# Second cross-attention of a Perceiver block: two positions at a time on 32-row and 32-column groups of TensorE

## The reference

```python
def _L1_xattn_ref(x, context, Wq, Wkv, Wout, bout):      # x: (8, 64, 256), context: (8, 1024, 256)
    heads, dim_head = (16, 64)
    q = x @ Wq
    k, v = jnp.split(context @ Wkv, 2, axis=-1)
    q, k, v = map(split_heads, (q, k, v))
    mask = j_idx % n_q == i_idx                            # key j counts for position i if j % 64 == i
    sim = jnp.einsum('bhid,bhjd->bhij', q, k) * scale
    attn = jax.nn.softmax(jnp.where(mask, sim, max_neg), axis=-1)
    out = jnp.einsum('bhij,bhjd->bhid', attn, v)
    return out @ Wout + bout
```

## Time and profile before

| | us |
|---|---|
| three runs | 892.03, 895.23, 895.33 (median 895.23) |
| the profiled execution | 893.96 |
| its span | 892.1 |
| PE busy in it | 839.7 (94%) |
| VectorE, ScalarE, GpSimd busy | 508.0, 413.1, 105.5 |
| mean granted TensorE clock | 0.987 |

### The profile page before, as it was taken

One profiled execution on the slowest core, in us unless ns is written; L12 is line 12 of the kernel. 1 busy time (PEld: TensorE's weight loads), 2 busy tenths in 40 slices (PEclk: granted clock), 3 DMA queues, 4 the chain that ended last, 5 costly groups with the idle time before them and its releaser, 6 DMA issues.

```text
span 892.1 us, 20057 instructions
## 1 busy us (share of the span) xinstructions
PE 839.7 (94%) x7916; PEld 681.3 (76%) x7916; DVE 508.0 (57%) x1181; ACT 413.1 (46%) x821; POOL 105.5 (12%) x102
## 2 busy tenths in 40 slices
PE   5999999999889798999999999999989999779997
PEld 3788788888748697888888888887369967568885
DVE  4777877787643655555555555554355631675332
ACT  3757566676640223445545454443455641422221
POOL 2333311340000440000000000000011000400200
PEclk9999999999999799999999999999999999989999
DMA  7446644476090000023123213004516668213860
GB/s 297 188 155 213 236 178 167 150 258 202 4 397 1 2 4 1 22 121 141 55 88 141 87 54 141 0 0 155 222 48 233 238 237 342 85 35 158 369 296 25
DMA packets 25867, 128.14 MB, mean 144 GB/s; under 512 B 2360, under 2 KB 8272, under 8 KB 21712
## 3 DMA queue, kind: packets, MB, share of 16 engines
q1 hardware_dynamic: 24624, 111.51, 33.4%
q0 software_dynamic: 1184, 15.77, 4.3%
HBM read 126.75 MB, written 0.52 MB: 143 GB/s over the span
## 4 chain that ended last, share of the span: by engine, by line
PE 82%; DVE 7%; DMA 4%; issue 2%; ACT 2%; SPq 1%; POOL 1%; DVEq 0%; ACTq 0%
PE PS L387 13%; PE PS L388 12%; PE PS L389 12%; PE PS L396 5%; PE PS L697 4%; PE PS L947 3%; DMA arena<-in_bias 3%; PE PS L1149 3%; PE PS L820 3%; PE PS L966 3%; PE PS L1161 3%; PE PS L709 3%; PE PS L686 3%; PE PS L935 2%; PE PS L920 2%
## 5 line engine op out<-in xcount | busy, mean ns | idle before, releaser
L1329 ACT CAST w_h<-arena 128x768 fp32r<-128x768 f32 x64 | 53.4, 835 | 124.8 <-PE PS L389 124.8
L1689 DVE TENSOR_TENSOR w_l<-arena,w_h 128x768 fp32r<-128x768 f32 x64 | 61.2, 957 | 87.0 <-ACT w_h L1329 87.0
L387 PE MATMUL PS<-xnT_h,w_h 128*128 128x512 f32 x256 | 99.7, 390 | 0.8 <-DVE xnT_l L381 0.8
L389 PE MATMUL PS<-xnT_h,w_l 128*128 128x512 f32 x256 | 99.6, 389 | 0.0
L388 PE MATMUL PS<-xnT_l,w_h 128*128 128x512 f32 x256 | 99.6, 389 | 0.0
L1527 DVE CUSTOM_DVE_ANT_0 arena<-PS,arena 128x512 f32<-128x512 f32 x128 | 86.9, 714 | 20.7 <-PE PS L686 18.7
L1229 ACT ACTIVATE arena<-arena 128x1024 f32<-128x1024 f32 x64 | 73.5, 1150 | 9.9 <-DVE arena L1527 9.8
L697 PE MATMUL PS<-consts,arena 128*128 128x128 f32 x512 | 68.3, 277 | 0.7 <-ACT arena L1234 0.4
L697 PEld LDWEIGHTS PS<-consts,arena 128*128 128x128 f32 x512 | 55.9, 141 | 10.5 <-issue 3.6
L1696 DVE TENSOR_TENSOR arena<-PS,arena 128x512 f32<-128x512 f32 x64 | 44.3, 691 | 29.1 <-PE PS L389 27.3
L387 PEld LDWEIGHTS PS<-xnT_h,w_h 128*128 128x128 f32 x256 | 48.0, 188 | 11.2 <-DVE xnT_l L381 1.2
(11 more groups left out here) (301 smaller groups left out, 1763.2 us busy)
## 6 DMA issues: line engine op xcount, KB each, us to landing
arena<-in_bias SPq DMA_DIRECT2D x64, 512.0 KB, 4.2
arena<-in_wall SPq DMA_DIRECT2D x8, 3072.0 KB, 9.9
arena<-in_wf SPq DMA_DIRECT2D x8, 2052.0 KB, 11.2
hT<-in_ctxT SPq DMA_DIRECT2D x12, 1024.0 KB, 6.4
arena<-in_ctxT SPq DMA_DIRECT2D x4, 1024.0 KB, 6.3
arena<-in_ctxG SPq DMA_DIRECT2D x4, 1024.0 KB, 4.8
hT<-in_ctxG SPq DMA_DIRECT2D x4, 1024.0 KB, 4.8
arena<-in_w SPq DMA_DIRECT2D x2, 1024.0 KB, 6.2
```

The costliest lines, as they stand in the source:

```text
L387: pe.matmul(out, a[0], b[0], start=start, stop=False)
L389: return pe.matmul(out, a[1], b[0], start=False, stop=stop)
L1329: act.copy(w_h[:, s % 4, :], stage[s // 8 % 2][:, s % 8, :]).then_inc(sem("c_wh"), 1)
L1689: dve.tensor_tensor(w_l[:, s % 4, :], stage[s // 8 % 2][:, s % 8, :], wide(w_h[:, s % 4, :]), ALU.subtract).then_inc(sem("c_wl"), 1)
```

## The change

- `U` is laid out as half, pair of positions, then 32 columns (16 heads x 2 positions), so that the queries of a pair of positions are 32 contiguous columns. `grouped`, `Ub` and `Ub0` go, on all three engines. The copies into `U` (L1725, L1367) now write runs of two words, and L989 reads such runs.
- `sims`: per batch 32 pairs x 2 halves = 64 products of 128 rows, 32 columns of the array and 32 keys. Four pairs in turn lie in the four column groups (output partitions 32j to 32j+31). The keys come from a new array `ctxD`, in which the 32 keys of a pair are contiguous.
- One mask and softmax for a batch: VectorE adds the mask `pair` (256 columns), takes maxima, subtracts; ScalarE exponentiates all 256 columns at once; VectorE sums, takes reciprocals, multiplies.
- `sums`: 2 transposes in place of 8, one copy of 256 columns, then 64 products with 32 rows each, in the four row groups, each into its own PSUM bank (4 to 7).
- `warm` products: 3 ahead of the first scores, 3 behind them, 6 ahead of the first sums and 4 ahead of each other batch's, 3 ahead of L989.
- The loops over batches are written out.
- SP loads `wq1`, `wkT1` and `wv1` behind the last expert's weights without waiting for the last expert; `wo1` waits as before. The self-attention's weights and the first five expert blocks are asked for after L989's last product.

```diff
-    U = cd(KC, XH, TOK)
+    U = [cd(B * PP, 2 * XH), None]
...
-            sp.wait_ge(sem("c_dn"), 4 + 8 * NEXP)
             w_in(wq1, A["wq1"], "in_wq1")
             w_in(wkT1, A["wkT1"], "in_wk1")
             w_in(wv1, A["wv1"], "in_wvo1")
+
+            sp.wait_ge(sem("c_dn"), 4 + 8 * NEXP)
             w_in(wo1, A["wo1"], "in_wvo1")
...
+            for b in range(B):
+                if b >= 2:
+                    sp.wait_ge(sem("d_sim"), b - 1)
+                sp.dma_start(ctxT1[b % 2], A["ctxD"][b].rearrange("(k p) n -> p k n", p=P))\
+                  .then_inc(sem(f"d_ctxT{b % 2}"), 16)
+                if b >= 2:
+                    sp.wait_ge(sem("d_w"), b - 1)
+                sp.dma_start(ctxG[b % 2], A["ctxG"][b]).then_inc(sem(f"d_ctxG{b % 2}"), 16)
+            sp.wait_ge(sem("d_o"), FC)
             w_in(wqkv, A["wqkv"], "in_wqkv")
             w_in(wproj, A["wproj"], "in_wqkv")
...
+            def sims(b):
+                pe.wait_ge(sem(f"d_ctxT{b % 2}"), b // 2 * 16 + 16)
+                if b >= 2:
+                    pe.wait_ge(sem("d_z"), b - 1)
+                for t in range(8):
                     for dc in range(KC):
+                        for j in range(4):
+                            pp = 8 * (t % 4) + 4 * (t // 4) + j
+                            last = pe.matmul(PS[32 * j:32 * j + 32, b % 2, 32 * t:32 * t + 32], U[dc][:, b * PP + pp, :],
+                                             ctxT1[b % 2][:, dc, 32 * pp:32 * pp + 32], start=dc == 0, stop=dc == KC - 1)
+                last.then_inc(sem("d_sim"), 1)
+
+            def sums(b):
+                pe.wait_ge(sem("d_p"), b + 1)
+                if b >= 2:
+                    pe.wait_ge(sem("d_te"), b - 1)
+                for t2 in range(2):
+                    last = pe.transpose(PS[:, 2, t2 * P:(t2 + 1) * P],
+                                        Z[:, b % 2, 4 * t2:4 * t2 + 4, :].rearrange("p a b -> p (a b)"), C("ident"))
+                last.then_inc(sem("d_t"), 1)
+                pe.wait_ge(sem(f"d_ctxG{b % 2}"), b // 2 * 16 + 16)
+                pe.wait_ge(sem("d_te"), b + 1)
+                if b:
+                    for dc in range(KC):
+                        pe.wait_ge(sem(f"d_we{dc}"), b)
+                for dc in range(KC):
+                    for t2 in range(2):
+                        for j in range(4):
+                            for r in range(4):
+                                k, at = slice(32 * r, 32 * r + 32), dc * D + (4 * t2 + j) * 32
+                                last = pe.matmul(PS[:, 4 + r, at:at + 32], ctxG[b % 2][k, 4 * t2 + j, dc * P:(dc + 1) * P],
+                                                 PTx[k, b % 2, t2, 32 * j:32 * j + 32], start=True, stop=True)
+                last.then_inc(sem("d_w"), 1)
+
+            for dc in range(KC):
+                pe.wait_ge(sem(f"d_ue{dc}"), 2 * FC)
+            warm(pe, 3, 3)
+            sims(0)
+            warm(pe, 3, 3)
+            for b in range(B):
+                if b + 1 < B:
+                    sims(b + 1)
+                warm(pe, 3, 6 if b == 0 else 4)
+                sums(b)
+            warm(pe, 3, 3)
...
             exps(0)
+            for b in range(B):
+                transposed(b)
+                if b + 1 < B:
+                    exps(b + 1)
+                summed(b)
...
             scores(0)
             probabilities(0)
+            for b in range(B):
+                if b + 1 < B:
+                    scores(b + 1)
+                    probabilities(b + 1)
+                summed(b)
```

More of the change, by code:

```diff
@@ L28 @@
 XH, XD = 16, 64
-GRP, GI = 8, 8
 GM = KEYS // S
+PP = S // 2
 EPS = 1e-5
@@ L46, in const_layout @@
         "half2": ((p % 32) // DK == np.arange(2)[None, :]),
-        "group": np.where(p % GI == c % GI, 0.0, -BIG),
+        "pair": np.where(p % 2 == np.arange(32)[None, :] % 2, 0.0, -BIG),
         "upper": i > j,
@@ L464, in _ @@
             sp.wait_ge(sem("a2_o"), 2)
-            with sp.Fori(0, NEXP // 2) as i:
+            for e2 in range(2):
+                sp.dma_start(stage[e2], A["wall"][e2:e2 + 1].rearrange("a p c n -> p (a c) n"))\
+                  .then_inc(sem(f"c_w{e2}"), 16)
+            with sp.Fori(1, NEXP // 2) as i:
                 for e2 in range(2):
@@ L495, in expert_in @@
                 sp.dma_start(wblk[e], A["wf"][e * P:(e + 1) * P]).then_inc(sem(f"f_w{e // 2}"), 16)
[L497 to L501, removed]
+            for e in range(5):
                 expert_in(e)
@@ L569, in _ @@
                     .then_inc(sem("b_pool"), 1)
[L571 to L588, removed]
+            pool.wait_ge(sem("d_w"), B)
             for n in range(2):
@@ L936, in _ @@
                                   start=True, stop=True).then_inc(sem(f"d_u{dc}"), 1)
[L938 to L961, removed]
-                    pe.wait_ge(sem("d_te"), b * 2 + hf + 1)
-                    for dc in range(KC):
-                        pe.wait_ge(sem(f"d_we{dc}"), b * 2 + hf + 1)
-                        for g in range(4):
-                            last = pe.matmul(PS[:, 4 + 2 * hf + dc, g * P:(g + 1) * P],
-                                             ctxG[j][:, 4 * hf + g, dc * P:(dc + 1) * P], PTx[:, hf, g, :],
-                                             start=True, stop=True)
-                        last.then_inc(sem("d_w"), 1)
@@ L984, in _ @@
+            pe.wait_ge(sem("d_we1"), B)
             for c in range(FC):
@@ L1372, in exps @@
             def exps(b):
-                for hf in range(2):
-                    act.wait_ge(sem("d_z"), b * 2 + hf + 3)
-                    for g in range(4):
-                        last = act.activation(Z[:, hf, g, :], Z[:, hf, g, :], ACT.Exp, bias=mx1[:, hf, g:g + 1],
-                                              scale=-1.0, accum_out=rs1[:, hf, g:g + 1])
-                    last.then_inc(sem("d_e"), 1)
+                act.wait_ge(sem("d_z"), b + 1)
+                z = Z[:, b % 2].rearrange("p a b -> p (a b)")
@@ L1392, in _ @@
-            exps(0)
-            with act.Fori(1, B) as b:
-                transposed(b - 1)
-                exps(b)
-                summed(b - 1)
-            transposed(B - 1)
-            summed(B - 1)
+                act.wait_ge(sem("d_w"), b + 1)
+                for dc in range(KC):
+                    last = act.copy(U[dc][:, b * PP + 16:(b + 1) * PP, :].rearrange("p (r q) n -> p r (q n)", r=2),
+                                    PS[:, 6:8, dc * D:(dc + 1) * D])
+                last.then_inc(sem("d_we1"), 1)
@@ new lines, in probabilities @@
+            def probabilities(b):
+                z, total, inv = Z[:, b % 2], rs1[:, b % 2, :], ri1[:, b % 2, :]
+                dve.wait_ge(sem("d_e"), b + 1)
+                ch.step(dve.reduce_sum(total, z, axis=AX.X))
+                ch.step(dve.reciprocal(inv, total))
+                dve.tensor_tensor(z, z, bcast(inv, 2, (8, 32)), ALU.mult).then_inc(sem("d_p"), 1)
+            def summed(b):
+                dve.wait_ge(sem("d_w"), b + 1)
+                for dc in range(KC):
+                    last = dve.tensor_copy(U[dc][:, b * PP:b * PP + 16, :].rearrange("p (r q) n -> p r (q n)", r=2),
+                                           PS[:, 4:6, dc * D:(dc + 1) * D])
+                last.then_inc(sem("d_we0"), 1)
@@ L1933 @@
         "ctxT": ctx.transpose(0, 2, 1),
-        "ctxG": ctx.reshape(B, GM, GRP, GI, D).transpose(0, 1, 3, 2, 4).reshape(B, P, GRP, D),
+        "ctxD": ctx.reshape(B, GM, PP, 2, D).transpose(0, 4, 2, 1, 3).reshape(B, D, KEYS),
+        "ctxG": ctx.reshape(B, GM, 4, 8, 2, D).transpose(0, 2, 1, 4, 3, 5).reshape(B, P, 8, D),
         "wq0": t("L0_xattn_Wq"), "wk0": t("L0_xattn_Wk"), "wv0": t("L0_xattn_Wv"), "wo0": t("L0_xattn_Wo"),
```

114 lines of the change are left out of this document (24 added, 90 removed).

## The result

The changed kernel takes 920.3 us in the median of four runs (917.67 to 921.35), the kernel before beside it 895.28 (892.03 to 896.47). The ratio is 1.028, with an interval of 1.025 to 1.031. The forecast was 885.9 us, with a range of 881 to 902: faster by 9 us, where the kernel became slower by 25. The profiled execution of after has a span of 919.0 us against 892.1.

A forecast was written before the change was run, and what follows sets the result against it. PE was taken as the bound, busy for 94% of the span. The stage summed as 13.2 + 44.4 (six batches of 7.4) + 6.2 + 1.5 = 65.3 against 74.65 us, 9.3 less, giving 885.9 us; range 881 to 902.

The forecast's parts named there:

- Scores: Query-key products of a batch: 128 records at 8.6 ns, 1.1 us in place of 3.7.
- sums: Weighted sums of a batch: 32 rounds of four row groups loading at once, 3.55 us against 3.81 before.
- transposes: From transposes to sums in a batch, with ScalarE's copy uncovered: 0.87 us against 1.16 before.
- constants: Warm products on PE's path: 0.43 us each, four a batch 1.72 us, 43 in the stage 18.5 us.
- changes of shape: PE switching tile shape, two a batch outside of waits: 0.1 us each, an estimate, 0 to 0.2.
- floor per record: Rival: small score records cost about 30 ns whatever their size, scores 3.8 us a batch, 907 us; chance 0.09.
- loads not four abreast: Rival: full-width fp32 loads of the sums don't run four at once; two abreast 914 us, singly 970; chance 0.05.
- The granted clock falls: Rival: the sums' thin stream doesn't count as work, so PE drops to 1.2 GHz; 899 to 936 us; chances 0.13 and 0.04.
- milder form: Clock rival with one 3.4 us stretch at 1.2 GHz per batch: 13.6 us lost, 899 us; chance 0.13.
- Value products: L989 reading U in runs of two words: 0 us, upper bound 14 us at half rate (900 us, chance 0.05).
- floor of 7.1: Context loads: wake, issue and landing take 7.1 us, wanted after 7.4, so nothing is lost.
- Regrouping copies, VectorE, other loads: Regrouping copies go, only the first (1.1 us) was on the path; VectorE hidden with 4.8 us to spare; other loads nothing.

The follow-up runs named there:

- e1_wide96: Changed kernel with each product of the sums streaming up to 96 columns instead of 32, the extra ones overwritten: 915.9 us, ratio 1.021 to the kernel before.
- e12_loop_wide96: Changed kernel with TensorE's batches 1 to 6 as a hardware loop and the sums' moving operand widened to up to 96 columns: 903.2 us, ratio 1.009.
- e5_full_sums: Changed kernel with its new scores kept, sums back to 16 whole-array products a batch and all 43 constants out: 890.0 us, ratio 0.994.
- e9_order: e5_full_sums with the scores' context load moved ahead on SP's queue and batch 1's scores ahead of batch 0's transposes: 887.0 us, ratio 0.990.

## Why the prediction was wrong, point by point

- **Scores, sums, transposes, constants, changes of shape.** Right. In the loop without stalls and at full clock: sums 3.77 (forecast 3.55 and a change of 0.1), scores 1.23 (1.1 and 0.1; the 8.6 ns a record was picked between bounds of 7.4 and 16.4, and 9.6 came), constants 1.92 (1.72), transposes to sums 0.73 (0.87); 7.65 to 7.73 us a batch against 7.4. The rivals "floor per record" and "loads not four abreast" fall: the records of the scores come at 1.23/128 = 9.6 ns with their waits, and a round of four sums takes 3.77/32 = 118 ns. The Trainium skill (TensorE: Matmul & The Clock Gate, Wait — 56ns, not 53.3ns?) has 25 ns between starts however few the columns; over four tiles in turn the chip went below it.
- **"The granted clock falls".** This is the step that failed. The forecast gave it 0.17 and had one stretch of 3.4 us a batch as its milder form. 53.6 of 95.8 us were at 1.2 GHz, which cost up to 26.8 us; with the stream widened and the loop in place of written-out code, 3.4 us were. The forecast held against it the stretch from 804.1, where half the time is L1098's records of 8 columns; the other half there were full-size products of constants. The thin sums had no such company: 3.8 us of them in a row. The argument took a stretch that was mixed as proof for one that is not. The forecast had the mechanism, with too small a chance and too small a size, and left it out of the sum.
- **Writing out.** This had no term at all, and is the second step that failed. The forecast counts products and loads, and nowhere what it takes to bring the instructions in. Writing out put some 530 TensorE instructions in a batch (2154 products' records and as many loads in the stage, against 580 of either before) and had them fetched: 18 packets in the stage against 3. That cost 5.0 us of stalls in after. In e1_wide96, where the clock came back for 33 us, the stalls rose to 11.7 and the stage fell by only 7.0. With forecast 65.3, clock 26.8 and stalls 5.0 the stage would be at 97.1; it is at 95.8. Both added terms are upper bounds: time at half clock is not all doubled, and the stalls hold some of PE's own work.
- **Value products.** 0 was forecast, with 14 us as a bound; 2.0 measured, of which 1.4 to 1.9 are the runs of two words.
- **Context loads.** The floor of 7.1 was near: in the loop of e12_loop_wide96 a load that was asked for 0.44 us after the sums landed 7.0 us later, 0.2 us ahead of the scores that wanted it. In after landing took 8.1 to 8.4, and none is on the chain, since its batches took 10 us and more. For a landing of 8 the forecast wrote 0.3 us a batch, where its own terms give 0.1 + 0.4 + 8 - 7.4 = 1.1. Only in e5_full_sums did the loads bind.
- **Regrouping copies, VectorE, other loads.** As forecast, none appears on the chain; VectorE is busy for 30.57 us of the stage.
- **Ahead of the stage.** 5 us in the profiled run that no term had; open.

## What to carry over

Price a rewrite not only by its products but by its instructions: on TensorE at full clock, written-out code of small products can outrun the fetch of its instructions, and a hardware loop whose body is reused does not. Judge the clock by what PE streams and not only by how busy a row says it is, and by a stretch that holds nothing but the new kind of work. Before giving up on such a change, keep the part that gained (here the scores) and put back the one that did not (the sums): that version, with its loads in a better order, ran at 0.988 to 0.991 of the kernel before.

## What the runs showed of the hardware

- A stall of TensorE of 0.45 to 4 us at multiples of 256 instructions, in the written-out code of the changed kernel and of all made from it; none in the later turns of a loop of about 1070 instructions.
- Products of constants can cost more than their own time: 3.4 us of them cost 9 us (886.5 against 895.7), with more stalls (13.4 against 10.1 us) and less time at 1.2 GHz (10.2 against 17.1).
- The clock fell to 1.2 GHz behind 3.40 us in which PE was busy for 2.93, all with products of 32 rows and 32 columns under loads of 128; with up to 96 columns and no stalls it stayed at 2.4 GHz, for the same 3.77 us a batch. The wider stream took no time of its own. The clock also fell behind 3.40 us with the new scores and a stall (busy for 1.30), in e9_order, which has no such sums.
- Runs of two fp32 words as a moving operand, at full clock: 14.8 to 15.3 us against 13.4 with adjacent words, for 64 records of 512 columns, first start to last.
